# First cross-attention of a decoder kernel: weighed rows copied earlier on ScalarE, ternary weight sizes spread over GpSimd and VectorE

## What is computed

```python
x = _layernorm(x + _L0_attn_ref(x, ...))                 # gated scan
x = _layernorm(x + _L0_xattn_ref(x, ctx, ctx, mask, bias, Wq, bq, Wk, bk, Wv, bv, Wo, bo))
x = _layernorm(x + _L0_ffn_ref(x, weight, gamma, beta))
...                                                      # three more steps

def _L0_xattn_ref(query, key, value, mask, chemical_bias, ...):   # 16 heads of 16
    scores = jnp.einsum('bhqd,bhkd->bhqk', q, k) / SCALE + chemical_bias[:, None, :, :]
    scores = jnp.where(mask == 0, -jnp.inf, scores)
    attn = jax.nn.softmax(scores, axis=-1)
    out = jnp.einsum('bhqk,bhkd->bhqd', attn, v)
    return out.transpose(0, 2, 1, 3).reshape(B, S, D) @ Wo.T + bo

def _ternary_quant_weight(w):                            # inside _L0_ffn_ref
    absw = jnp.abs(w)
    delta = THRESHOLD * jnp.mean(absw)
    mask = (absw > delta).astype(w.dtype)
    alpha = jnp.sum(absw * mask) / jnp.maximum(jnp.sum(mask), 1.0)
    wq = alpha * jnp.sign(w) * mask
```

## Time and profile before

| | us |
|---|---|
| median of 3 runs | 827.79 |
| lowest, highest | 825.74, 828.64 |
| the profiled execution | 827.26 |
| its span in the trace | 825.5 |

### The profile page before, as it was taken

The page is one execution under the profiler, slowest core; times in us unless marked ns, Lnnn a source line. Parts: engine busy times, 40 slices in busy tenths (PEclk is TensorE's granted clock), DMA queues, the critical chain, the costliest instruction groups (busy, mean ns, idle before and its releaser), DMA issues.

```text
span 825.5 us, 20952 instructions
## 1 busy us (share of the span) xinstructions
PE 779.8 (94%) x6901; PEld 596.4 (72%) x6901; DVE 649.5 (79%) x2458; ACT 615.8 (75%) x1602; POOL 427.8 (52%) x461
## 2 busy tenths in 40 slices
PE   9998899999988988999999999999999999999996
PEld 7876677777666766677777777777676777677786
DVE  3997778888998867688777767775888888986777
ACT  4547898888884367888888887885999999984331
POOL 0265465667845145553555544225865666335764
PEclk9999999999999999999999999999999999999999
DMA  9401661222101458988989889865122222100001
GB/s 314 151 26 39 199 204 37 85 84 85 72 15 71 185 177 246 302 244 267 272 239 283 257 250 280 267 184 179 43 69 69 68 69 69 66 1 1 23 30 52
DMA packets 105393, 115.05 MB, mean 139 GB/s; under 512 B 29061, under 2 KB 94085, under 8 KB 105030
## 3 DMA queue, kind: packets, MB, share of 16 engines
q1 hardware_dynamic: 104724, 113.35, 43.5%
q10 hardware_dynamic: 562, 0.35, 0.1%
HBM read 48.09 MB, written 51.82 MB: 121 GB/s over the span
## 4 chain that ended last, share of the span: by engine, by line
PE 49%; ACT 7%; DVE 5%; issue 2%; DMA 1%; POOL 1%; SPq 0%; DVEq 0%; ACTq 0%
PE bank L1563 7%; PE bank L242 6%; PE bank L2327 6%; PE bank L250 5%; PE bank L2344 3%; PE bank L2313 3%; PE bank L1578 3%; PE bank L1614 3%; PE bank L1604 3%; PE bank L1547 2%; PE bank L2379 2%; ACT Sx L1770 2%; PE bank L2361 1%; PE bank L234 1%; ACT q_heads L1778 1%
## 5 line engine op out<-in xcount | busy, mean ns | idle before, releaser
L242 PE MATMUL bank<-x_feat,w_all_mats 128*128 128x256 f32 x384 | 93.4, 388 | 1.9 <-ACT q_full L358 0.6
L242 PEld LDWEIGHTS bank<-x_feat,w_all_mats 128*128 128x128 f32 x384 | 70.7, 192 | 14.8 <-ACT rw L2702 3.8
L2660 ACT ACTIVATE bias_area<-bias_area,mq_two 128x256 f32<-128x256 f32 x128 | 66.6, 536 | 0.0
L3056 POOL TENSOR_TENSOR bnd<-bnd,consts 128x60 f32<-128x60 f32 x64 | 18.5, 311 | 81.1 <-DMA bnd<-band_scratch 81.0
L3045 POOL COPY rw<-rw 128x856 f32<-128x856 f32 x32 | 29.0, 905 | 57.9 <-ACT rw L2702 57.9
L894 ACT ACTIVATE dist<-dist,mq_two 128x256 f32<-128x256 f32 x128 | 56.1, 503 | 3.5 <-DVE mq_two L1005 3.5
L2836 DVE COPY q_heads<-bank 128x512 f32<-128x512 f32 x64 | 41.7, 685 | 21.1 <-PE bank L2327 21.1
L1770 ACT ACTIVATE Sx<-Sx,mq 128x256 f32<-128x256 f32 x128 | 54.3, 501 | 2.3 <-DVE mq L1868 2.3
L1876 DVE COPY q_heads<-bank 128x512 f32<-128x512 f32 x64 | 42.1, 685 | 17.0 <-PE bank L1563 17.0
L1005 DVE CUSTOM_DVE_ANT_0 dist<-bank,bias_area 128x256 f32<-128x256 f32 x128 | 46.5, 420 | 10.7 <-PE bank L701 5.6
L1770 ACT ACTIVATE Pr<-Pr,mq 128x256 f32<-128x256 f32 x128 | 54.5, 505 | 0.0
(11 more groups left out here) (322 smaller groups left out, 2377.9 us busy)
## 6 DMA issues: line engine op xcount, KB each, us to landing
dist<-skew_scratch SPq DMA_DIRECT2D x64, 296.0 KB, 4.2
skew_scratch<-rw SPq DMA_DIRECT2D x30, 588.0 KB, 5.2
bnd<-band_scratch SPq DMA_DIRECT2D x64, 108.0 KB, 2.7
band_scratch<-bias_area SPq DMA_DIRECT2D x32, 162.0 KB, 3.3
band_scratch<-bias_area SPq DMA_DIRECT2D x32, 148.0 KB, 2.6
skew_scratch<-dist SPq DMA_DIRECT2D x4, 1024.0 KB, 8.4
context_values<-dist SPq DMA_DIRECT2D x8, 512.0 KB, 2.6
v_two<-context_values SPq DMA_DIRECT2D x8, 512.0 KB, 4.2
```

Of the source, the lines that this page charges most:

```text
L242: last = pe.matmul(dst[:, m * S:(m + 1) * S], w[:, k, m * P:(m + 1) * P], rhs[:, k, :], start=(k == 0), stop=(k == FT - 1))
L2660: last = act.activation(rows_of(n, g)[:, t, :], rows_of(n, g)[:, t, :], ACT.Exp, bias=mq_two[:, n % 2, g, t:t + 1], scale=-1.0, accum_out= ...
```

## The change

There are two parts.

The first is on ACT. `copy_ot(4b - 1)`, for b = 1 to 7, no longer stands at the head of the second round of batch b; it stands in the first round, between `exps(n + 1, 2)` and `exps(n + 1, 3)`.

The second concerns `ternary_sum`. The negation `wneg = -W` is made by POOL (`ternary_opposite`), at the end of POOL's batch 6. The rest of `ternary_sum` moves on DVE from behind the norm of batch 6 into the last round, between the two copies `turned(31, 0)` and `turned(31, 2)`. The sizes and the mask now lie in the places of the two weight matrices `x0_Wq` and `x0_Wk`, which are done with by then, since `Pr` is still in use in the last round. `w_step.n = 1` counts the step that POOL has taken.

```diff
-        wneg, absw, wmask = q_full[:, :, :], Pr[:, 0, :, 0:S], Pr[:, 1, :, 0:S]
+        wneg, absw, wmask = q_full[:, :, :], W["x0_Wq"][:, :, :], W["x0_Wk"][:, :, :]
...
                             more = n + 1 < NQ * B
-                            if n >= 2:
+                            if n >= 2 and j != 1:
                                 copy_ot(n - 2)
...
                             if more:
                                 exps(n + 1, 2)
+                            if j == 0 and b >= 1:
+                                copy_ot(n - 1)
+                            if more:
                                 exps(n + 1, 3)
...
                     def ternary_sum():
 
-                        dve.wait_ge(t_mm, 4 * NQ * B)
-                        dve.wait_ge(q_split, FT * B)
-                        w_step(dve.tensor_scalar(wneg, W_ffn[:, :, :], -1.0, None, ALU.mult))
+                        dve.wait_ge(k_sb, B)
+                        w_step.n = 1
                         w_step.wait()
                         w_step(dve.tensor_tensor(absw, W_ffn[:, :, :], wneg, ALU.max))
...
                                 peaks(n + 1, 3)
+                            if not more:
+                                ternary_sum()
                             turned(n, 2)
...
                     dve.memset(v_stage[:, :, :, DH:DH + 1], 1.0).then_inc(stage_made, 1)
-                    ternary_sum()
                     fold_peak(B - 3)
...
+                    def ternary_opposite():
+
+                        pool.tensor_scalar(wneg, W_ffn[:, :, :], -1.0, None, ALU.mult).then_inc(w_steps, 1)
...
                             split_q(b + 2)
                             split_k(b + 2)
+                        if b == B - 2:
+                            ternary_opposite()
```

## The result

| | before | after |
|---|---|---|
| median, us (runs) | 827.56 (4) | 820.74 (4) |
| lowest, highest | 825.74, 828.64 | 820.36, 821.59 |
| profiled execution | 827.26 | 820.36 |
| its span | 825.5 | 818.6 |

The ratio is 0.9921, with a 95% interval from 0.9902 to 0.9941: the kernel is 0.8% faster, 6.8 us by the medians and 6.9 by the profiled executions. The prediction was 820.8. The kernel before has one run more here than at the prediction (827.56 in place of 827.79).

A forecast was written before the change was run, and what follows sets the result against it. PE, busy 94%, was taken to set the pace of the first cross-attention, so gains lie in its waits: 5.4 us from the copy plus 1.4 from the sizes, 6.8 off, gives 820.8 us, range 818.8 to 824.3.

The forecast's parts named there:

- The wait on line 747 falls from 0.96 to 0.17 us, seven times.: Batches 1 to 7: PE's wait for ACT's copy before turn_back shrinks to about 0.17 us, as the copy starts 0.79 earlier.
- 6 x 0.79 + 0.63 = 5.4 from the rounds: Moved copy: six batches gain 0.79 us each, batch 7 only 0.63 by DVE's idle time; bounds 0 and 6.8 us.
- All three engines are at their limit at 0.79: Rounds of a batch: PE, DVE and ACT can each follow by 0.79 us and no further, DVE with 0.01 to spare.
- rival A: Rounds: a small unseen overlap gives part of the gain back, about half (2.7 us) arrives, time 823.5 us; chance 0.14.
- Part 2 brings 1.4 us: Tail: PE's 1.47 us wait for w_stats at line 866 goes, less 0.1 for the port; bounds 0 and 1.5 us.
- 0.1 us off for the port in the tail: Tail: DVE's mask loses about 0.24 us beside POOL's second TENSOR_SCALAR pair, mostly covered by 0.26 of slack at the end.
- The sizes lose 0.4 us in the last round, covered by 1.1 of room: Last round: DVE's two-input sizes lose about 0.4 us beside POOL's TENSOR_SCALARs; the second copy may come 1.1 us late.
- The rule of two exclusive sides: Shared DVE-POOL port: by it the mask would wait up to 1.22 us, losing 0.85 us of the second part, not 0.1.
- Negation on POOL at nothing: POOL, batch 6's end: the negation takes 1.57 us inside 3.72 us of idle time, so it costs nothing.
- C: First rounds: ACT stands still waiting for PE's weighing, seven batches lose 0.52 us each, about 830 us; chance 0.03.
- D: Before turn_back: another semaphore, the values' copy, holds it at nearly the same time, 826 us; 0.06 with a larger give-back.
- B: Last round: the sizes wait for POOL's run to end, weigh(31) starts 1.5 us late, time 822.2 us; chance 0.08.

The follow-up runs named there:

- e1_copy_alone: The kernel before with only ACT's copy moved between the last two groups of exponentials, the sizes left in place: median 822.86 us, ratio 0.9921 to 0.9952.
- e3_copy_first: The changed kernel with ACT's copy ahead of both last groups of exponentials of the first round: median 819.28 us, ratio 0.9897.
- e9_split_group: The changed kernel with the copy one exponential earlier, between the two of group 2: median 820.62 us, ratio 0.9887 to 0.9926.
- e7_own_bank: The changed kernel with the last weighing, weigh(31), in a PSUM bank of its own: median 821.32 us, ratio 0.9912 to 0.9938.
- e5_negate_on_vector: The changed kernel with the negation back on DVE, in the last round ahead of the sizes: median 820.56 us, ratio 0.9904 to 0.9932.
- after_again: The changed kernel measured once more, unaltered: median 820.93 us, ratio to the kernel before 0.9892 to 0.9922.
- e10_first_and_bank: The changed kernel with the copy ahead of both last groups of exponentials and weigh(31) in its own bank: median 820.09 us, ratio 0.9886 to 0.9918.

## Why the prediction was right, point by point

- *The wait on line 747 falls from 0.96 to 0.17 us, seven times.* It did: 1.2 us in all, 0.17 in batch 3.
- *6 x 0.79 + 0.63 = 5.4 from the rounds.* Measured 5.48, by e1_copy_alone 5.52. The seventh batch brought 0.71 and not 0.63, the idle time of the earlier trace rows: the difference is the 0.08 us row that reads DVE's accumulator, with which the reciprocal now starts together (both at 236.66 us; next point).
- *All three engines are at their limit at 0.79.* This step was wrong, at no cost for this change. ACT and PE had room, and DVE had 0.09 us beyond its shown idle time of 0.80, since an operation can start together with the 0.08 us row ahead of it. e3_copy_first and e9_split_group gained 0.1 us a batch more. The thin margin, the main argument for rival A, was thus wider than it looked.
- *Part 2 brings 1.4 us.* It brought 1.74. The wait was 1.47; I had left out that PE goes from one matmul to the next without a gap. From the start of line 250 to line 866 it took 3.46 us with the wait and 1.83 without, 0.16 more than the wait, and from line 866 to `turn_back(7, 0)` 0.25 and 0.14. That is 1.47 + 0.16 + 0.11 = 1.74.
- *0.1 us off for the port in the tail.* The mask's two steps lost 0.37 us, not 0.24, yet nothing arrived at the end: line 884 is 7.65 us sooner, as `turn_back(7, 0)` is. Before, and after, in the timeline of DVE:

```profile
264.02 0.69 DVE L1144 TENSOR_TENSOR Pr<-Pr 128x512 f32<-128x512 f32 x1
```
```profile
254.97 2.59 POOL L1299 TENSOR_SCALAR x_tok<-y_sb,mv,rstd 128x256 f32<-128x256 f32 x2
...
255.85 0.63 DVE L1144 TENSOR_SCALAR w_all_mats<-w_all_mats,ffn_scalars 128x512 f32<-128x512 f32 x1
...
256.51 0.92 DVE L1146 TENSOR_TENSOR w_all_mats<-w_all_mats 128x512 f32<-128x512 f32 x1
```

- *The sizes lose 0.4 us in the last round, covered by 1.1 of room.* They lost nothing (0.68 us); their cover was not needed. DVE began them 0.38 us ahead of POOL's first TENSOR_SCALAR, and it was POOL that lost: 1.41 us for that one, 1.22 for the next. The second copy came at 249.33, 5.92 us ahead of 255.25 and so in step with everything else.
- *The rule of two exclusive sides.* The Trainium skill, page "SBUF — State Buffer", section "SBUF: two separate sides", would have the loser blocked for the whole of the other's instruction. By it the one that starts first gets the port. The runs agree for POOL's TENSOR_TENSOR of 128x512: DVE's operation took 1.66 us against 0.68, and ended about its own length after POOL's. They differ for POOL's TENSOR_SCALAR where that one is first: the mask's second step began at 256.51, 0.33 us behind POOL's second TENSOR_SCALAR (256.18 to 257.56), took 0.92 us against 0.69 and ended ahead of it. In e7_own_bank the mask's first step began 0.11 us behind POOL's and took 0.71 us against 0.49. The sizes of the last round say nothing on this, since DVE came first there. Nor were the 0.85 us that the prediction put on the rule worked out: 1.22 less the slack of 0.26 is 0.96.
- *Negation on POOL at nothing.* Right for the stage, 1.50 us measured against 1.57, and shown by two more of them. That it had to leave DVE was an assumption that I didn't test in the prediction: e5_negate_on_vector shows that its place was the cost. And leaving DVE cost 0.37 us at the end of the program, a term that the prediction did not have.
- *Rivals.* A, C and D are refuted by the rows above. B's outcome did not come (0.68 us, nothing late), but its condition, POOL first at the port, did not occur either, so what it would have cost stays untested. The scans that the prediction set against B lay beside POOL's TENSOR_SCALARs too, and the rows of the mask point the same way. C's wait exists in e3_copy_first (ACT idles 0.43 us before the copy), and that kernel gains rather than loses.

The mechanisms of both parts were right. That the number is so close is luck in part: the sum was 0.1 and 0.3 us too small inside the stage, the start gave 0.43, and 0.38 and 0.37 were lost behind it. For part 2 alone, 1.74 - 0.37 is just the 1.4 that was predicted, for another reason.

## What to carry to other kernels

Where an engine copies a result that the critical engine waits for, look at what it does between the result and the copy. Work whose consumer comes later goes behind the copy, and a short wait of that engine for its input costs nothing if its own queue has room: each batch got back the length of what stood in front. How much arrives is read from the idle time of the engine that takes the next step, in the same round, and that number held to 0.1 us here. Before moving an expensive operation to another engine, see what lies beside it: the same negation took 2.25, 0.42 and 1.50 us by its place and engine, and the move to the other engine lost more behind the stage than it gained inside.

## What the runs showed of the hardware

I had not expected TensorE's clock to play a part. At the stage's end PE has a few tiny matmuls (lines 882, 884 and 886) and then stands still for 1.1 us, which the trace puts down to PE's own sequencer. In five of the twelve profiled executions of the changed kernels the granted clock then fell to half, 1.2 GHz, and in the others it stayed at 2.4. The changed kernel itself did both. Busy time and granted clock of PE in stretches of 3 us, first execution:

```profile
272.00:275.00 3.00, 1.89 (x14) 1.00 0.54 162
275.00:278.00 3.00, 2.81 (x18) 1.00 0.19 70
278.00:281.00 3.00, 3.00 (x18) 1.00 0.00 0
```

Second execution (after_again):

```profile
272.00:275.00 3.00, 1.91 (x14) 0.89 0.49 141
275.00:278.00 3.00, 3.00 (x10) 0.50 0.11 39
278.00:281.00 3.00, 3.00 (x10) 0.50 0.00 0
```

The same four matmuls of line 2581, in the first and in the second:

```profile
275.45 1.08 PE L2581 MATMUL bank<-w_all_mats,aT 128*128 128x256 f32 x4
```
```profile
275.24 2.02 PE L2581 MATMUL bank<-w_all_mats,aT 128*128 128x256 f32 x4
```

What PE did before the fall was the same in both: the row after the pause, of after_again, is

```profile
273.07 1.75 PE L2577 MATMUL bank<-ident 128*128 128x128 f32 x12 [1.11 <-PEq L679]
```

and its pause of 1.11 us is that of the first execution to 0.01. So the order of the instructions doesn't decide it. The fall cost 3.0 us in after_again and in e7_own_bank (the shift against before went from 8.04 to 5.04, and from 8.48 to 5.40), and 1.3 in e1_copy_alone, e5_negate_on_vector and e10_first_and_bank. 3.0 us is more than most of what is told apart in this study, and it may be why the medians of e1_copy_alone and e7_own_bank lie above what their stage gains promise; only one execution of each has a trace, so that is argued and not shown. The mean granted clocks of the other executions don't settle it: of the changed kernel, 821.59 us went with 0.998 and 820.62 with 0.995. What triggers it stays open: I have no run in which only the pause was changed. The other differences between executions are smaller: in the first 7 us, 0.41 between the two of the changed kernel and 1.3 between the earliest and the latest of all thirteen, and up to 0.9 us where later stages wait for transfers.

Whoever compares kernels that differ by about 1 us should therefore compare the distances between events inside the stage that was edited, where two executions agreed to 0.02 us, and not the whole time. The 0.37 us behind the last matmul shows what that misses: one look at the rest of the trace belongs to it.
